# A scan over state items: the chunk's preparation spread over two passes

## What is computed

```
h = layernorm(x) * (1 + scale) + shift             # per sequence, from the conditioning
xm, z = split(h @ W_in)                            # 512 and 512
xm = silu(causal_conv4(xm) + conv_b)               # 4 taps, per channel
dtr, B, C = split(xm @ W_xp)                       # 64, 16, 16
dt = softplus(dtr @ W_dt + b_dt)
state = state * exp(dt * A) + (dt * xm) * B        # 512 x 16, for every step in turn
y = (sum over the 16 states of state * C + xm * D) * silu(z)
out = x + gate * (y @ W_out)
```

## Time and profile before

| | us |
|---|---|
| median of 3 runs | 2338.38 (2334.12 to 2338.6) |
| the profiled execution | 2334.89 |
| its span | 2333.1 |

### The profile page before, as it was taken

How to read it: one execution, slowest core, us unless ns; L and a number is a source line. 1 busy time by engine, 2 the same in 40 slices (tenths; PEclk the granted TensorE clock), 3 DMA queues, 4 the chain that set the end, 5 groups by cost and what they waited for, 6 DMA issues and landing times. The chain is left out here.

```text
span 2333.1 us, 44474 instructions
## 1 busy us (share of the span) xinstructions
PE 2051.4 (88%) x13497; PEld 1579.0 (68%) x13497; DVE 1969.4 (84%) x3686; ACT 1688.3 (72%) x3652; POOL 1635.2 (70%) x1800
## 2 busy tenths in 40 slices
PE   4899999995699999999999999999999999999870
PEld 3566666662467777777777777777777778777760
DVE  2788888884299898989889898989989898988983
ACT  0455555552688888898888879898888979888840
POOL 2799999985667676776767677776767677676530
PEclk8999999996699999999999999999999999999995
DMA  5122212211000000000000000000000000000218
GB/s 142 39 64 64 64 62 63 62 49 36 10 1 19 6 15 6 15 15 6 15 5 19 6 15 8 13 15 6 20 6 15 6 15 15 6 6 6 95 69 288
DMA packets 71471, 80.75 MB, mean 35 GB/s; under 512 B 12227, under 2 KB 63619, under 8 KB 69188
## 3 DMA queue, kind: packets, MB, share of 16 engines
q1 hardware_dynamic: 66052, 69.52, 9.3%
q10 hardware_dynamic: 5184, 8.39, 1.0%
HBM read 44.33 MB, written 33.55 MB: 33 GB/s over the span
## 5 line engine op out<-in xcount | busy, mean ns | idle before, releaser
L632 ACT ACTIVATE decay<-dtT,decay_rate 128x256 f32<-128x256 f32 x2048 | 866.5, 495 | 0.2
L527 PE MATMUL bank<-ident,decay 128*128 128x128 f32 x4096 | 622.4, 275 | 101.6 <-ACT decay L632 56.0
L537 PEld LDWEIGHTS bank<-ident,scaled 128*128 128x128 f32 x4096 | 486.2, 142 | 231.6 <-issue 193.1
L537 PE MATMUL bank<-ident,scaled 128*128 128x128 f32 x4096 | 622.8, 275 | 1.5 <-POOL scaled L452 1.4
L527 PEld LDWEIGHTS bank<-ident,decay 128*128 128x128 f32 x4096 | 471.7, 141 | 143.7 <-ACT decay L632 103.7
L452 POOL TENSOR_SCALAR scaled<-state,bc 128x512 f32<-128x512 f32 x384 | 278.2, 730 | 255.9 <-DVE state L752 209.3
L742 DVE TENSOR_TENSOR bank<-bank,state 128x512 f32<-128x512 f32 x512 | 340.8, 691 | 117.7 <-PE bank L527 111.5
L452 POOL TENSOR_SCALAR scaled<-fresh,bc 128x512 f32<-128x512 f32 x384 | 273.5, 717 | 235.0 <-DVE fresh L752 214.3
L742 DVE TENSOR_TENSOR bank<-bank,fresh 128x512 f32<-128x512 f32 x512 | 340.3, 690 | 58.9 <-PE bank L527 55.4
L752 DVE SCALAR_TENSOR_TENSOR fresh<-dtx,bc,bank 128x512 f32<-128x512 f32 x512 | 356.9, 737 | 0.0
L752 DVE SCALAR_TENSOR_TENSOR state<-dtx,bc,bank 128x512 f32<-128x512 f32 x512 | 356.8, 737 | 0.0
(11 more groups left out here) (139 smaller groups left out, 3617.0 us busy)
## 6 DMA issues: line engine op xcount, KB each, us to landing
xt<-in_x_dram SPq DMA_DIRECT2D x64, 128.0 KB, 2.2
resid<-x SPq DMA_DIRECT2D x64, 128.0 KB, 1.8
normed<-xh SPq DMA_DIRECT2D x64, 128.0 KB, 1.7
xg<-normed SPq DMA_DIRECT2D x64, 128.0 KB, 2.1
ssm_out<-yo SPq DMA_DIRECT2D x32, 256.0 KB, 2.0
fin_r<-resid SPq DMA_DIRECT2D x8, 1024.0 KB, 13.2
mask_bc<-in_mask_BxS_ik_dram SPq DMA_DIRECT2D x64, 64.0 KB, 2.9
fin_y<-ssm_out SPq DMA_DIRECT2D x32, 128.0 KB, 3.0
```

The costliest lines, as they stand in the source:

```text
L527: mm = pe.transpose(dec_bank[i % DECAY_BANKS][:, m * P:(m + 1) * P], decay[:, i // BLOCK % 2, n % GROUP, m, t % HALF * P:(t % HALF + 1) * ...
L537: mm = pe.matmul(y_bank[t % HALF][:, m * P:(m + 1) * P], scaled[:, i % RING, m * P:(m + 1) * P], ident[:, :], is_transpose=True, start=Fal ...
L632: act.activation(decay[:, block % 2, e // CB, m, :], dtT[par][:, m, half * HTOK:(half + 1) * HTOK], ACT.Exp, scale=decay_rate[:, m, n:n + ...
```

## The change

- The preparation of a chunk now covers two passes before its scan: h, u and the first half of the conv stand in the pass of chunk c-2 (position 0 to 63 of the table), the rest of the conv, dtr, dt, z, bc and x in that of chunk c-1 (`B1`), the last two x in its own (`B2`). There is one more body ahead of chunk 0. The order of banks is counted from the table.
- `SLOTS` is new: pieces of u and z stand at every second slot or in pairs with a gap, the products of dt between those of z, out0 at slots 61 to 63, out1 at 9 to 11.
- All twelve tap pairs of a chunk are on GpSimd, one instruction a slot in slots 45 to 63 and 0 to 4. VectorE has none.
- z is no longer copied. ScalarE takes tanh from the bank into zs, and VectorE computes (tanh + 1) · z with z still in the bank, and so frees it. GpSimd's z gating is gone.
- The tanh of x goes into dtT and no longer into tmp.
- dtr is two pieces of two products, on 64 columns each; its halves are added by a w_dt that stands twice on 128 rows. B and C are made turned (bcT, four products on 32 columns each), moved by ScalarE, and turned and added by four small products with eye_sum (bc).
- `ON_SCALAR` names items and no longer states: every fourth item in the order of the scan.
- The Ln stands at slot 37, the softplus steps at 39 to 46, the carry at 9, the modulation at 14 and 18. SyncE's gather of chunk c+3 follows h1 of chunk c+2.

```diff
-ON_SCALAR = (3, 7, 11, 15)
+ON_SCALAR = tuple(range(3, 64, 4))
...
+        SLOTS = {"dtr": at(B1, 7, 14), "out1": at(B3, 9, 10, 11), "dt0": at(B1, 17), "z0": at(B1, 18, 19),
+                 "bcT": at(B1, 20, 21), "dt1": at(B1, 22), "bc": at(B1, 24, 25), "z1": at(B1, 26, 27),
+                 "dt2": at(B1, 28), "z2": at(B1, 30, 31), "dt3": at(B1, 32), "z3": at(B1, 34, 35),
+                 "h0": at(0, 37), "h1": at(0, 39), "u0": at(0, 41, 43), "u1": at(0, 45, 47), "u2": at(0, 49, 51),
+                 "u3": at(0, 53, 55), "out0": at(B2, 61, 62, 63),
+                 "x0": at(B1, 57), "x1": at(B1, 59), "x2": at(B2, 2), "x3": at(B2, 5)}
+
+        POOL_TAPS = [(m, k) for m in range(CB) for k in range(TAPS - 1)]
+        POOL_TAP_SLOTS = at(45, *range(2 * len(POOL_TAPS)))
+        X_ORDER, X_TANH, X_GATE = (0, 1, 2, 3), (57, 61, B1 + 3, B1 + 9), (59, 63, B1 + 5, B1 + 11)
+        MOVE_AFTER = {"dtr": 2, "bcT": 2, "z1": 2, "z2": 2, "z3": 2}
+        MODULATE, CARRY, LN = at(0, 14, 18), B1 + 9, B1 + 37
+        SOFTPLUS = at(B1, *range(39, 39 + 2 * CB))
+        Z_GATES = at(B1, 20, 28, 32, 36)
+        ROWS = {"out1": B3 + 12, "out0": B3 + 0}
+        BODIES = range(-2, CHUNKS + 1)
+
+        def chunk_at(c, i, position):
+
+            k = c + 2 - position // ITEMS
+            return k if position % ITEMS == i and 0 <= k < CHUNKS else None
...
+                    pe.wait_ge(s_xs, k * CB + 2 * piece + 2)
+                    for g in range(P // DTR):
+                        m = X_ORDER[2 * piece + g]
+                        mm = pe.matmul(side[g * DTR:(g + 1) * DTR, :], w_xp[:, m, 0:DTR], x[:, m, :],
+                                       start=(piece == 0), stop=(piece == pieces - 1), skip_group_check=True)
+                elif kind == "bcT":
+                    for g in (2 * piece, 2 * piece + 1):
+                        mm = pe.matmul(side[g * 2 * DS:(g + 1) * 2 * DS, :], w_xp[:, g, DTR:DTR + 2 * DS],
+                                       x[:, g, :], start=True, stop=True, tile_position=(0, g * 2 * DS))
                 elif kind == "bc":
-                    t = piece
+                    if piece == 0:
+                        moved(pe, k, "bcT")
+                    for t in (2 * piece, 2 * piece + 1):
+                        mm = pe.matmul(side[:, t * 2 * DS:(t + 1) * 2 * DS], bcT[:, t * P:(t + 1) * P], eye_sum[:, :],
+                                       start=True, stop=True)
...
                 if kind == "z":
-                    ins = act.activation(zs[1 - par][:, k, :], side[:, :], ACT.Copy)
+                    act.activation(zs[k % 2][:, b, :], side[:, :], ACT.Tanh, scale=0.5).then_inc(s_ztanh, 1)
+                    return
...
+            def gate_z(k, b):
+
+                ve.wait_ge(s_ztanh, k * CB + b + 1)
+                side, z = side_turn(k, f"z{b}")[0], zs[k % 2][:, b, :]
+                ve.scalar_tensor_tensor(z, z, 1.0, side_bank[side][:, :], ALU.add, ALU.mult)\
+                    .then_inc(s_side_moved[side], 1)
```

More of the change, by code:

```diff
@@ new lines, in build @@
+        BODIES = range(-2, CHUNKS + 1)
+        def chunk_at(c, i, position):
+            k = c + 2 - position // ITEMS
+            return k if position % ITEMS == i and 0 <= k < CHUNKS else None
+        SEQUENCE, COMPLETED = {}, {}
+        for c in BODIES:
+            for i in range(ITEMS):
+                for job in SLOTS:
+                    first, last = chunk_at(c, i, SLOTS[job][0]), chunk_at(c, i, SLOTS[job][-1])
+                    if first is not None:
+                        SEQUENCE[job, first] = len(SEQUENCE)
+                    if last is not None:
+                        COMPLETED[job, last] = len(COMPLETED)
@@ L346, in scalings @@
         def scalings(on_scalar, i):
-            return sum((item_of(k)[0] in ON_SCALAR) == on_scalar for k in range(i))
+            return sum((k in ON_SCALAR) == on_scalar for k in range(i))
         def scaled_item(eng, c, i):
@@ L399, in prefetch_resid @@
                         .then_inc(s_fin_r, 16)
-            def body(c, par, post, scan, pre):
-                if pre and c + 2 < CHUNKS:
-                    filled(sp, c, "h1")
-                    apart(sp)
-                    gather(c + 2)
-                if post:
+            for c in BODIES:
+                if scanned(c - 1):
                     store_rows(c - 1, 1)
@@ L517, in mamba_tensor @@
+            for c in BODIES:
+                for i in range(ITEMS):
+                    slot(c, i)
         def mamba_tensor(pe):
@@ L618, in mamba_tensor, with slot @@
-            mamba_bodies(pe, body)
+            SKIPS = [index_of(0, t) + LAG - 1 for t in range(T)]
+            def slot(c, i):
+                if i + 2 < ITEMS:
+                    if scanned(c):
+                        turn_decay(c, i + 2)
+                elif scanned(c + 1):
+                    turn_decay(c + 1, i + 2 - ITEMS)
+                if scanned(c) and i in SKIPS:
+                    skip_term(c, SKIPS.index(i))
+                for job in SLOTS:
+                    for piece, position in enumerate(SLOTS[job]):
+                        k = chunk_at(c, i, position)
+                        if k is not None:
+                            fill(k, job, piece)
+                if i >= LAG and scanned(c):
+                    sum_state(c, i - LAG)
+                if i < LAG and scanned(c - 1):
+                    sum_state(c - 1, i - LAG + ITEMS)
@@ new lines, in slot @@
+            def slot(c, i):
+                for e in (2 * (i % BLOCK), 2 * (i % BLOCK) + 1):
+                    if i // BLOCK + 1 < BLOCKS:
+                        if scanned(c):
+                            make_decay(c, i // BLOCK + 1, e)
+                    elif scanned(c + 1):
+                        make_decay(c + 1, 0, e)
+                if i < 2 and scanned(c - 1) and i - 2 + ITEMS in ON_SCALAR:
+                    scale_state(c - 1, i - 2 + ITEMS)
+                if i >= 2 and scanned(c) and i - 2 in ON_SCALAR:
+                    scale_state(c, i - 2)
+                for job in SLOTS:
+                    k = chunk_at(c, i, SLOTS[job][-1] + MOVE_AFTER.get(job, 1))
+                    if k is not None and job[:3] != "out":
+                        move(k, job)
+                for step, position in enumerate(X_TANH):
+                    k = chunk_at(c, i, position)
+                    if k is not None:
+                        x_tanh(k, step)
+                k = chunk_at(c, i, LN)
+                if k is not None:
+                    softplus_log(k)
```

440 lines of the change are left out of this document (182 added, 258 removed).

## The result

The changed kernel takes 2260.3 us (median of 4 runs, 2257.5 to 2263.5) where the kernel before takes 2336.3 (2331.8 to 2338.6) on the same chip: a ratio of 0.968, 95% interval [0.966, 0.970]. It is faster, by 3.2%. The forecast was 2191 us, and 2260 lies 5 us above the range that I gave. The profiled execution spans 2261.8 us; its busy times are PE 1991, DVE 1930, ACT 1663 and POOL 1622 us (PE 2051, DVE 1969, ACT 1688 and POOL 1635 before). So TensorE has 60 us less to do, and the span is 71 us shorter.

The account below looks back on a forecast made before the run. TensorE bounds one half of a pass and VectorE the other, each wasting the other's spare time. From 2334.9 us, 152.6 (14 x 10.9) and 14.4 off, 19 and 1 on: 2187.9, plus 3.5 to the median, 2191; range 2160 to 2255.

Parts of the forecast that it names:

- TensorE's work, 92.0 us a pass: TensorE's products in a pass: cheaper dtr and dt bring 95.6 us to 92.0, with column groups fully overlapping.
- Rival 1: Column groups do not overlap in the scan: +3.5 us a pass, 96.5, 2240 us; chance 0.12.
- VectorE's work, 89.7: VectorE's demand in a pass: six taps go, four z gates of 0.6 us come, 89.7 us.
- The Ln "costed at nothing": Ln moved to slot 37: no TensorE stall, by a 1 us margin; without it the old 1.8 us returns.
- GpSimd's lag covered "with 1 us left": GpSimd's lag of 9 us in slots 39 to 60 is covered by LAG, decay banks and early start; 1 us left.
- a sign of being wrong: The prediction is wrong if GpSimd's scalings release TensorE's sums in every pass.
- rival 2: GpSimd bounds slots 39 to 68: 95.6 us a pass, 2228 us; with late x tanhs 97, 2247; chance 0.14.
- rival 3: The hand-off of z banks or the Ln stall returns: 96.8 us a pass, 2245 us; chance 0.08.
- x gates + 0.5 us a pass: VectorE's x gates, three in or at the edge of GpSimd's taps, cost 0.5 us a pass for collisions.
- Rival 4: VectorE's x gates wait out GpSimd's taps: 3.2 us more on VectorE, some 95 a pass, 2219 us; chance 0.05.
- Slower: GpSimd's taps cost some 3.6 us a pair: 110.6 us a pass, 2440 to 2460 us; chance 0.04.
- The front, +19: Before the scan's first item: chunk 0's taps all on GpSimd and other moved work add 19 us, bounds +11 and +27.

Follow-up runs that it names:

- e17: e3 with all four x gates as one-operand copies as in e15, parts of the computation left out: 2171.8 us, 0.930 of the kernel before.
- e1: Changed kernel with the Ln replaced by a Copy of the same width, so no table loads in mid-pass: 2246.0 us, 0.962 of the kernel before.
- e7: Changed kernel with twelve identity transposes filling TensorE's idle before the wait for item 43's decays: 2250.1 us, 0.963 of the kernel before.
- e2: Changed kernel with the first of GpSimd's three tap pairs of every block cut from 512 to 16 columns: 2230.7 us, 0.955 of the kernel before.
- e3: Changed kernel with the edits of both e1 and e2: 2192.6 us, 0.939 of the kernel before.
- e15: Changed kernel with all four x gates as one-operand copies of the tanh, gating by x left out: 2231.9 us, 0.957 of the kernel before.
- e10: Changed kernel with the scalings of items 43, 47, 51, 55 and 59 on GpSimd instead of ScalarE: 2371.7 us, 1.015 of the kernel before.

## Why the forecast missed, point by point

**TensorE's work, 92.0 us a pass: held.** dtr 1.08 for my 1.15, bcT 1.05, bc 0.53, dt 1.02 listed (0.87 to the next start), and e17, with both stalls and the collisions gone, runs at 92.6 with TensorE 99% busy. Rival 1 is out. (The terms of the first sum make 95.3, not 95.6, so that 91.7 would have followed.) The Trainium skill (TensorE: Matmul & The Clock Gate, Why this matters for your kernels) gives three 32-column products together 2.38 times the rate of one, less than a full overlap; the trace shows a full one for two column groups of 32 (1.05 us). The 0.2 us that the prediction made of that figure does not follow from it: 3 / 2.38 is 1.26, by estimate 0.9 us on four pieces of 0.87.

**VectorE's work, 89.7: held.** In e17 it is busy 1243.5 / 1285 of 92.6, 89.6 us. The z gates cost what was said; VectorE waits for two of them (0.6 and 0.5 us a pass, for ScalarE's tanh) and is not late for it.

**The Ln "costed at nothing": the step failed, and did not set the time.** I put TensorE at u0 10.0 us after the start of VectorE's pair 36 and the move of h1 at 9.0. Both were off, and the 1 us between them is gone:

```profile
1481.99 1.29 DVE L748 TENSOR_TENSOR bank<-bank,fresh 128x512 f32<-128x512 f32 x2
1491.80 0.58 ACT L642 ACTIVATE hT<-bank 128x512 f32<-128x512 f32 x1
```

h1 is moved 10.4 us after that start, and TensorE is through with what it can do of slot 41 after 7.7 (1489.7), so that it would be at u0 after 8.2. The old stall of 1.8 us came back as 2.0, as the condition that I had set beside the step says, with a fall of the clock that I did not foresee. Of this only the clock counts, 0.75 us a pass (e1, e7).

**GpSimd's lag covered "with 1 us left": this is the step that failed.** The row was priced well (49 us of work in 50.8, the taps unstretched); its cover was not. GpSimd's scalings release TensorE's sums in every pass, which I had named as a sign of being wrong. With this row as the limit and the clock up a pass takes 97.0 to 97.2 (e1, e7), the upper end of what rival 2 gave, 97. With the Ln's stall alone it takes 96.0 (e2, 96.2 with the clock's falls; rival 3 gave 96.8), without either 93.8 (e3; the forecast 93.0). So the pass is the largest of three limits, 97.1, 96.0 and 93.8, plus 0.75 for the clock. Rival 2's upper end alone comes to 2247 us, within the range; the clock's 10 us and the 8 us more in the front are what carried the time beyond its end.

**x gates + 0.5 us a pass: mis-sized.** They take 1.04 us in the median and 1.93 at most, and cost 1.2 us a pass with both stalls gone (e3 against e17) and 1.4 in the changed kernel as it is (e15, less the clock), there by GpSimd's row. The rule that I had weighed lightly, that the pair of ports is taken for a whole instruction and the loser waits (the Trainium skill, SBUF — State Buffer, Terms), was the better guide than the median of the kernel before. There 42 of 56 gates stood beside a GpSimd instruction as well, but the loser was mostly GpSimd: a gate takes 0.68 us and the tap's multiply beside it 1.64. I had looked for the collision on VectorE's side only. Rival 4 has the right mechanism.

**Slower.** The rival named 3.0 us a pair as the point from which it decides. (By its own sum 103.5 a pass is 2338 us, not 2345.) e10 shows that it was nearer than that: with a pair still at 2 us, 3.3 us of scalings in the row put the kernel at 2372, 1.5% slower than before, by the gate that doesn't get in and the clock behind it.

**The front, +19: mis-sized, within its bounds.** Chunk 0's gates wait 6.3 us each for their three tap pairs, as said; the x gates of chunk 1 (639.5 and 646.6) then stand in front of item 0, and the first item starts at 647.2: +27, my upper bound.

## What to carry to other kernels

When two engines each stall the bound one once in a loop, price the loop as the largest of the rings, not as a sum of stalls, and test a fix to one with the other fixed as well: here either alone gave 1 to 2 us and both 4.1. A row of work on an engine that idles 25% of the time can still set the pass, if all of it stands between one hand-over and the next; spread it, or move its small pieces to where their engine idles. And before GpSimd's row is made denser where VectorE has to read two SBUF tensors, look at the longest of these instructions and not at the median: one of them took 11 us here.
